# A selective-scan and expert kernel: deeper product ring, spread row scatters, sums kept in the output, and products with zeros on TensorE

## The reference, cut to what matters

```
h = layernorm(x) * (1 + ca) + sa                       # x: 8 sequences x 512 tokens x 256
xn = h * rsqrt(mean(h*h) + eps) * norm_w
xi, z = split(xn @ W_in)                               # 512 channels each
xc = silu(causal_conv(xi, 4 taps) + conv_b)
dt, Bm, Cm = split(xc @ W_x)                           # 64, 16, 16
dt = softplus(dt @ W_dt + b_dt)
h_s[t] = exp(dt*A_s) * h_s[t-1] + dt*xc*Bm[:, s]       # 16 states s, a scan over the 512 tokens
y = sum_s h_s * Cm[:, s] + D_skip * xc
x = x + ga * (h + (y * silu(z)) @ W_out)
h = layernorm(x) * (1 + cb) + sb
w, idx = top_2_of_8(h @ Wg), softmaxed
out_e = relu(xhat_e @ W1_e + b1_e) @ W2_e + b2_e + h   # only the two chosen experts count
x = x + gb * sum_of_two(w * out_e)
```

## Time and profile before

| what | value |
|---|---|
| median of three runs | 1634.65 us |
| profiled execution | 1636.39 us, span 1634.1 us |
| PE, DVE, POOL, ACT busy, share of the span | 81%, 76%, 65%, 48% |
| scan stage (73 to 1161 us): DVE busy | 958.7 of 1088 us |
| late tiles (1200 to 1600 us): PE busy | 397.2 of 400 us |

### The profile page before, as it was taken

The page is one execution under the profiler, slowest core; times in us unless marked ns, Lnnn a source line. Parts: engine busy times, 40 slices in busy tenths (PEclk is TensorE's granted clock), DMA queues, the critical chain, the costliest instruction groups (busy, mean ns, idle before and its releaser), DMA issues.

```text
span 1634.1 us, 25818 instructions
## 1 busy us (share of the span) xinstructions
PE 1329.9 (81%) x7954; PEld 1081.0 (66%) x7954; DVE 1237.3 (76%) x2161; ACT 786.4 (48%) x1378; POOL 1054.4 (65%) x942
## 2 busy tenths in 40 slices
PE   4567786777777887887888788778799999999994
PEld 1245465455556665665666566767689999999993
DVE  3798999989979889889998987789355555555552
ACT  2666768757857766775776586476000000000000
POOL 2485887998797898889789687978324352212221
PEclk7797998998989989889888988889999999999997
DMA  6212131321233344334144132944957797667664
GB/s 224 68 52 76 51 56 53 110 74 57 91 103 104 89 145 110 99 112 139 66 120 143 43 108 97 260 149 130 332 158 201 205 270 206 203 201 200 204 185 138
DMA packets 129471, 221.83 MB, mean 136 GB/s; under 512 B 17052, under 2 KB 74920, under 8 KB 129080
## 3 DMA queue, kind: packets, MB, share of 16 engines
q1 hardware_dynamic: 110376, 186.34, 37.3%
q0 software_dynamic: 16064, 28.53, 7.2%
q10 hardware_dynamic: 2896, 5.31, 1.1%
HBM read 182.79 MB, written 41.54 MB: 137 GB/s over the span
## 4 chain that ended last, share of the span: by engine, by line
PE 41%; DVE 20%; POOL 15%; issue 11%; ACT 8%; DMA 2%; SPq 1%; DVEq 0%; POOLq 0%; ACTq 0%
PE psum L1673 12%; PE psum L1689 12%; POOL dBu L873 10%; DVE w_sb L1974 10%; PE psum L1491 5%; DVE y L1985 3%; PE psum L1500 2%; ACT psum L1125 2%; POOL gT L727 2%; POOL rows_d L791 2%; PE psum L1629 2%; ACT hc L1109 1%; PE psum L1642 1%; PE psum L1480 1%; DVE xc L1955 1%
## 5 line engine op out<-in xcount | busy, mean ns | idle before, releaser
L873 POOL TENSOR_TENSOR dBu<-w_sb,brep 128x512 f32<-128x512 f32 x512 | 650.9, 1345 | 65.4 <-DVE w_sb L1974 54.1
L1974 DVE TENSOR_TENSOR_SCAN w_sb<-psum,dBu 128x512 f32<-128x512 f32 x512 | 612.0, 1210 | 93.8 <-ACT psum L1125 46.0
L1491 PE MATMUL psum<-ident,w_sb 128*128 128x128 f32 x2048 | 312.0, 301 | 153.2 <-DVE y L1985 101.1
L1125 ACT ACTIVATE psum<-w_sb,aneg 128x512 f32<-128x512 f32 x512 | 347.6, 692 | 179.3 <-DVE w_sb L1974 176.4
L1491 PEld LDWEIGHTS psum<-ident,w_sb 128*128 128x128 f32 x2048 | 253.3, 154 | 232.2 <-DVE y L1985 144.3
L860 POOL DMA_INDIRECT sum_d<-dBu,token x59 | 92.3, 1564 | 307.7 <-DVE dBu L2196 286.1
L1109 ACT ACTIVATE hc<-psum,ct 128x512 f32<-128x512 f32 x256 | 174.7, 682 | 114.8 <-PE psum L1491 87.4
L1500 PE MATMUL psum<-ident,hc 128*128 128x128 f32 x1024 | 178.1, 308 | 47.8 <-ACT hc L1109 36.4
L1500 PEld LDWEIGHTS psum<-ident,hc 128*128 128x128 f32 x1024 | 138.5, 159 | 92.3 <-ACT hc L1109 62.9
L1985 DVE SCALAR_TENSOR_TENSOR y<-psum,ct,y 128x512 f32<-128x512 f32 x240 | 174.2, 726 | 14.1 <-PE psum L1491 13.7
L1673 PE MATMUL psum<-xgT,win 128*128 128x128 f32 x960 | 112.2, 275 | 1.8 <-issue 1.8
(11 more groups left out here) (264 smaller groups left out, 1758.2 us busy)
## 6 DMA issues: line engine op xcount, KB each, us to landing
brep<-b_d SPq DMA_DIRECT2D x128, 256.0 KB, 3.6
win<-in_W SPq DMA_DIRECT2D x30, 1024.0 KB, 5.0
expert_pieces<-in_W SPq DMA_DIRECT2D x29, 1024.0 KB, 5.0
expert_pieces<-in_W SPq DMA_DIRECT2D x42, 512.0 KB, 5.2
dBu<-rows_d SPq DMA_DIRECT2D x35, 257.0 KB, 2.8
w_sb<-in_W SPq DMA_DIRECT2D x8, 1024.0 KB, 12.9
xg<-rows_d SPq DMA_DIRECT2D x22, 257.0 KB, 2.8
h_d<-hmod SPq DMA_DIRECT2D x8, 512.0 KB, 2.9
```

The costliest lines, as they stand in the source:

```text
L873: nc.gpsimd.tensor_tensor(dBu[:, i % RING, :], u[p][:, c, :], brep[:, s % 4, :], ALU.mult).then_inc(s_dBu, 1)
L1125: nc.scalar.activation(dA[:, i % DA_RING, :], dt[p][:, c, :], ACT.Exp, scale=aneg[:, c, s:s + 1]).then_inc(s_dA, 1)
L1491: last = nc.tensor.transpose(T[:, i // DT, c * P:(c + 1) * P], hs[s % 2][:, c, i * P:(i + 1) * P], ident[:, :])
L1974: nc.vector.tensor_tensor_scan(hs[s % 2][:, c, :], dA[:, i % DA_RING, :], dBu[:, (n * UNITS + i) % RING, :], 0.0, ALU.mult, ALU.add).then_ ...
```

## The change

It has four parts.

1. `RING` goes from 6 to 9.
2. POOL's `send_rows` of a sequence is spread. Two of the eight scatters stood at the end of step 15 and six in steps 0, 1 and 2. Now two stand in each of steps 0, 1, 4 and 5. The early `tile_out` of step 4 goes to step 6. On SP, `load_gate` goes from step 6 to step 9, and for n = 3 `tile_rows` from step 6 to step 7.
3. The tensor `sum_d` is gone. Bases are stored into `out`, and the accumulating scatters go to `out` with a bounds check that drops the filling rows. The last copies, and the zeroing of the spare rows at the start, are gone.
4. PE issues `add_zeros(count)`: float32 products of a 128x128 block of zeros with 512 columns of ones, which are added to PSUM bank 7. They stand at two places of a step, ahead of `states(n, s, 1)` and ahead of `add_up(n, s, 1)`, wherever `occupied` says that the step holds no other matmul there. Counted over the program there are 212 of them: 40 for n = 0, 34 each for n = 1 and 2, 20 each for n = 3 to 6, and 24 for n = 7.

```diff
-RING = 6
+RING = 9
@@ SP
-                sp.dma_start(rows(sum_d, n), x1[:, :, :]).then_inc(s_bast, 16)
+                sp.dma_start(rows(out, n), x1[:, :, :]).then_inc(s_bast, 16)
-                    if 3 <= n <= 6 and s == 6:
+                    if 3 <= n <= 6 and s == (7 if n == 3 else 6):
                         tile_rows(t)
                         tile_pieces(t, (0, 1, 2))
-                    if n >= 1 and s == 6:
+                    if n >= 1 and s == 9:
                         load_gate(n - 1)
-                for n in range(0, NB, 2):
-                    store_out(sp, n)
-                sp.wait_ge(s_out, 16 * NB)
+                sp.wait_ge(s_bast, 16 * NB)
@@ POOL
-                pool.indirect_dma_start(sum_d, bass.IndirectOffsetOnAxis(ap=token[:, i % XR:i % XR + 1], axis=0),
-                                        ysl[:, i % YR, :], None, compute_op=ALU.add).then_inc(s_st, 16)
+                pool.indirect_dma_start(out, bass.IndirectOffsetOnAxis(ap=token[:, i % XR:i % XR + 1], axis=0),
+                                        ysl[:, i % YR, :], None, bounds_check=NTOK - 1, oob_is_err=False, compute_op=ALU.add).then_inc(s_st, 16)
...
                     if n >= 2 and s == 0:
+                        send_rows(n - 2, 0, (0, 1))
+                    if n >= 2 and s == 1:
                         send_rows(n - 2, 0, (2, 3))
-                    if n >= 2 and s == 1:
+                    if n >= 2 and s == 4:
                         send_rows(n - 2, 1, (0, 1))
-                    if n >= 2 and s == 2:
+                    if n >= 2 and s == 5:
                         send_rows(n - 2, 1, (2, 3))
-                    if 4 <= n <= 7 and s == 4:
+                    if 4 <= n <= 7 and s == 6:
                         tile_out(t - 1)
...
-                    if has_o and s == 15:
-                        send_rows(n - 1, 0, (0, 1))
@@ ACT
-                act.wait_ge(s_st, 16 * TILES)
-                for n in range(1, NB, 2):
-                    store_out(act, n)
@@ PE
+            def add_zeros(count):
+                for i in range(count):
+                    nc.tensor.matmul(YT[:, DT + 1, :], zeros[:, :], ones[:, :].unsqueeze(1).to_broadcast([P, DT * 2, P]),
+                                     start=False, stop=False, skip_group_check=True)
+            def occupied(n, s, second):
+                has_o, has_p, has_t = n > 0, n < NB - 1, 3 <= n <= 6
+                if second:
+                    return (has_o and s in (2, 3, 4) or has_p and s in (7, 12, 13) or has_t and s in (6, 8, 14, 15)
+                            or n == NB - 1 and s in (2, 3, 5, 6, 10, 11, 13, 14))
+                return (has_p and s in (2, 3, 4, 5, 8, 12, 13) or has_t and s in (7, 9, 15)
+                        or n == NB - 1 and s in (3, 4, 6, 7, 11, 12, 14, 15))
...
+                    if s > 1 and not occupied(n, s, False):
+                        add_zeros(2)
                     states(n, s, 1)
...
+                    if s > 0 and not occupied(n, s, True):
+                        add_zeros(4 if s == 5 else 2)
                     if s > 0:
                         add_up(n, s, 1)
```

More of the change, by code:

```diff
@@ L62, in adaln_kernel @@
     h_d = dram("h_d", (NTOK, D))
-    sum_d = dram("sum_d", (NTOK + P, D))
     ctx = ExitStack()
@@ L81, in adaln_kernel, with program @@
         YT = psum[:, 4:8, :]
-        program(nc, ctx, sem, ident, tab, psum, T, dA, Q, MOD_PS, YT, mod_d, b_d, h_d, rows_d, sum_d, out,
+        program(nc, ctx, sem, ident, tab, psum, T, dA, Q, MOD_PS, YT, mod_d, b_d, h_d, rows_d, out,
                 x, norm_w, W_in, conv_w, conv_b, W_x, W_dt, b_dt, A_log, D_skip, W_out, Wg, cT, wmod,
                 gamma, beta, W1, b1, W2, b2)
-def program(nc, ctx, sem, ident, tab, PS, T, dA, Q, MOD_PS, YT, mod_d, b_d, h_d, rows_d, sum_d, out,
+def program(nc, ctx, sem, ident, tab, PS, T, dA, Q, MOD_PS, YT, mod_d, b_d, h_d, rows_d, out,
             x, norm_w, W_in, conv_w, conv_b, W_x, W_dt, b_dt, A_log, D_skip, W_out, Wg, cT, wmod,
@@ L169, in program @@
         lower = sb("lower", [P, P])
+        zeros = sb("zeros", [P, P])
         ones = sb("ones", [P, P])
@@ L205, in program @@
         m8n = gT[0:NB, 0, 0:2 * D].rearrange("p (a d) -> p a d", a=2)
-        zrow = hc[:, 0, 0:D]
         def two_of(t):
@@ L212, in program @@
         xs_of = [xin[:, :, :], two_of(xc)[0], *two_of(u), *two_of(dt), *two_of(sz)]
-        s_zero = sem("spare_rows_zeroed")
         s_w = sem("weights_loaded")
@@ L330, in program @@
         s_yb = sem("late_tile_y_with_bias")
-        s_out = sem("out_stored")
         X0_PS = PS[:, 0:4, :]
@@ L415, in expert_on @@
             return eng.value_load(tab[0:1, 0, t:t + 1], min_val=0, max_val=E - 1)
-        def store_out(eng, n):
-            eng.dma_start(out[n * L:(n + 1) * L, :].rearrange("(p i) d -> p (i d)", p=P),
-                          sum_d[n * L:(n + 1) * L, :].rearrange("(p i) d -> p (i d)", p=P)).then_inc(s_out, 16)
         block = own.enter_context(nc.Block())
@@ L566, in prologue @@
                 sp.wait_ge(s_modst, 32)
-                sp.wait_ge(s_const, 1)
-                sp.dma_start(sum_d[NTOK:NTOK + P, :], zrow).then_inc(s_zero, 16)
                 store_h(1)
@@ L657, in _ @@
         def _(pool):
-            pool.memset(zrow, 0.0)
             pool.memset(mhalf[:, :], -0.5)
@@ L662, in _ @@
             pool.memset(used[:, :], 0.0)
+            pool.memset(zeros[:, :], 0.0)
             for k in range(2):
@@ L851, in tile_out @@
                 after(pool, s_st, 16 * t)
-                pool.indirect_dma_start(sum_d, bass.IndirectOffsetOnAxis(ap=idx[:, t % 2:t % 2 + 1], axis=0),
-                                        ysb[:, :], None, compute_op=ALU.add).then_inc(s_st, 16)
+                pool.indirect_dma_start(out, bass.IndirectOffsetOnAxis(ap=idx[:, t % 2:t % 2 + 1], axis=0),
+                                        ysb[:, :], None, bounds_check=NTOK - 1, oob_is_err=False, compute_op=ALU.add).then_inc(s_st, 16)
             def late_out(t):
@@ L946, in epilogue @@
                 tile_out(BEGIN - 1)
-                send_rows(NB - 2, 0, (2, 3))
                 gate(NB - 1, 1)
+                send_rows(NB - 2, 0)
                 send_rows(NB - 2, 1)
@@ L999, in store_base @@
                 act.wait_ge(s_base, n + 1)
-                act.dma_start(sum_d[n * L:(n + 1) * L, :].rearrange("(i p) d -> p i d", p=P), x1[:, :, :]).then_inc(s_bast, 16)
+                act.dma_start(out[n * L:(n + 1) * L, :].rearrange("(i p) d -> p i d", p=P), x1[:, :, :]).then_inc(s_bast, 16)
             def mod_copy(j):
@@ L1278, in prologue @@
                     z_first(c)
-                act.wait_ge(s_zero, 16)
             def body(n, p, has_o, has_p, has_r):
```

## The result

The changed kernel takes 1662.22 us (median of four runs, 1656.06 to 1665.77), the kernel before 1636.2 us in the runs beside it. The ratio is 1.0163, 95% interval 1.0138 to 1.0188: **26 us slower**, where 52 us faster was forecast (1583 us) and even the range ended at 1606. The execution of the trace took 1665.77 us, the longest of the four.

A forecast was written before the change was run, and what follows sets the result against it. DVE's last scan was taken to end the scan stage, with 101 us of its waits to win; PE bounds the late stage. 1636.4 - 14.5 - 22 - 15 = 1584.9 us for the profiled execution, so 1583 us, range 1560 to 1606.

The forecast's parts named there:

- part 3: End of the span: without the last copies the kernel ends after the last scatter lands, 14.5 us less.
- parts 1 and 2: Scan stage: deeper ring and moved scatters cut DVE's 27.3 us of waits behind POOL, 22 us less.
- part 4: Scan stage: products with zeros raise PE's clock and shorten DVE's waits behind PE, net 15 us less.
- The checked scatter: Late stage: the bounds check was taken at no cost; 1.55 us on POOL, about 4.0 us to land.
- Rival D: Late stage: a checked scatter link takes longer than a late tile's 7.25 us; about 1687 us at 9 us; chance 0.04.
- at full clock they fit: Scan stage: 212 products with zeros take 106 us at full clock, where PE has 237 us free.
- rival C: Scan stage: PE becomes the bound, products with zeros delay DVE by 0.9 us a place, 1693 us; chance 0.06.
- The clock: Scan stage: PE's mean granted clock, 0.89 before, should be above 0.95.
- the mechanism: Scan stage: products with zeros hold the clock up, and DVE's 28.1 us of waits behind PE shrink by 16.
- the sign that I had named for a false mechanism: Scan stage: the clock rises and DVE's waits behind PE, 28.1 us before, don't shrink.
- the stalls of the earlier trace: Scan stage: DVE waits behind PE at half clock, one of 3.00 us in step 6 of sequence 3.
- taken off a fifth: Scan stage: of DVE's 27.3 us behind POOL, a fifth was taken off for DVE then waiting on ACT, leaving 22.

The follow-up runs named there:

- run 10: The whole changed kernel, products with zeros included, with the residual's first half kept in PSUM: 1638.48 us, ratio 0.9998 to the kernel before.
- run 7: The changed kernel with each product with zeros on 128 columns, not 512; number and places kept: 1616.24 us, ratio 0.9854 to the kernel before.
- run 11: The kernel before with spread scatters, the end's change, ring of six, residual's first half in PSUM and quarter-length products with zeros: 1606.31 us, ratio 0.9818.
- run 39: Not a run's label but a count: the unchanged kernel before was run 39 times beside the experiments; 1636.2 us in the runs beside the changed kernel.
- run 3: The kernel before with only the end's change (sums kept in `out`, checked scatters, no last copies); ring of six, old scatters: 1624.9 us, ratio 0.9925.
- run 1: The changed kernel without its 212 products with zeros: 1616.53 us, ratio 0.9891 to the kernel before.
- run 6: As run 1, with the residual's first half kept in PSUM, so the addition has one SBUF input: 1609.15 us, ratio 0.981.
- run 12: As run 3, with the residual's first half kept in PSUM: 1622.14 us, ratio 0.9916 to the kernel before.
- run 9: The kernel before with the end's change, a ring of nine, old scatters and the residual's first half in PSUM: 1621.18 us, ratio 0.9898.
- run 2: The kernel before with only the 212 products with zeros added: 1679.47 us, ratio 1.0258.

## Why the prediction was wrong

The terms as the runs have them are -12 (part 3), -8.4 (parts 1 and 2) and +45.7 (part 4), where the sum had -14.5, -22 and -15. Nearly all of the miss is part 4.

**Part 3, right.** -14.5 us in the trace; 12 in the runs.

**The checked scatter, right.** It takes 1.55 us and lands in 4.0 in the median, as before, and a late tile still takes 7.25 us. Rival D did not happen.

**Part 4, the step that failed**: "A 128x512 float32 product takes 1.98/4 = 0.5 us at full clock". The `x4` in the earlier trace rows counts records, and a float32 product leaves two. I had the means to see it: the half of an early tile (L1629) stands as `x8` in the order of PE and as `x16` in the earlier trace rows, and the output projection as `x4` in that order and as `x8` in the trace of before:

```profile
647.82 1.89 PE L1523 MATMUL psum<-wout,gT 128*128 128x256 f32 x8
```

So the price is 0.94 us a product at full clock, and 206 us in the stage (412 records, the rest lies outside) instead of 106. The sum counted 1 us of cost for this, since "at full clock they fit". Free time of PE over a stage says nothing on that: PE is busy 937 of 1088 us, so time is still free, and yet the products delayed the transposes that ACT and DVE wait for. The measured cost is 45.7 us on 106 pairs, 0.43 us a pair. (They stand at 99 places, not 106, since seven places have two pairs.) That is rival C, which put the point where nothing is left at 0.35 us a pair, and which I gave 0.06. Its condition, "if the clock stays at 0.5", was wrong with the same factor of two: at full clock a pair already takes 1.9 us. And its sign, PE busy over 1000 us in the stage, did not show.

**The clock.** Forecast above 0.95 in the stage; it was 0.94, and 0.96 in run 10. The first half of the mechanism (products with zeros raise the clock) holds. The second (DVE's waits behind PE shrink with it, 16 us) does not: together they went from 28.1 to 33.7 us (4.0 for the scan, 29.7 for y), which is the sign that I had named for a false mechanism. Runs 7 and 11 have a clock higher by 0.03 at a third of the PE time and gain nothing that can be told from zero. Of the stalls of the earlier trace rows, the first stood at full clock in the changed kernel and was no shorter (3.45 us), and the second stood again beside a fallen clock (3.28). What a rise of the clock alone would be worth stays open, since both runs change the clock and PE's work together. It may be more than nothing. The kernel before was run 39 times beside the experiments, its clock over the whole span lay between 0.900 and 0.916, and the time went against it: the 12 executions at 0.913 or more took 1629.8 to 1637.9 us, the 5 at 0.903 or less 1640.4 to 1643.7. Which is cause and which effect, these numbers don't say.

**Parts 1 and 2, half right.** Forecast -22 us, measured -8.4 (run 3 to run 1). The stalls behind POOL went (35.7 to 8.3 us), but the scatters did all of it, and I had let both share one sum. On top, the addition that the ring lengthens was a cost that I had no line for. From run 3 to run 1 it grew from 14.7 to 25.2 us for 14, and taking the hold away (run 6) gives 7.4 us back. The rest is missing without it too: with the residual in PSUM, parts 1 and 2 bring 13.0 us (run 12 to run 6), not 22. I had taken off a fifth for waits that turn into others. From run 3 to run 1 the DVE waits that PE ended, for scan and y, rose from 23.2 to 31.3 us, which may be that rest; it was not tested. In the changed kernel the 14 additions took 31.1 us, and in step 3 of sequences 3 to 6, from one `y` to that of the next step, 14.4 to 14.8 us, where the kernel before has 9.3 to 10.6 and run 10 has 9.3 in all four.

The trace of before held the sign. All 14 additions are of one shape, with a median of 691 ns and a longest of 1986, though no row names a wait inside them. A longest of three times the median is what I passed over. The Trainium skill, "SBUF — State Buffer", section "Who interferes with whom", says that a DVE instruction with two SBUF inputs and a GpSimd instruction that reads SBUF exclude each other, the later one blocked until the earlier has finished. The runs agree that it takes two SBUF inputs (0.69 us with one, run 9). But the rule as written would hold the addition for one product, 1.3 us. Here it took 6.07 us, beyond the end of a whole row of four, although it had started 0.6 us before that row.

The price of the zeros depends on the rest: 45.7 us with the residual in SBUF and 29.3 in PSUM (run 6 to run 10). One way is that a late TensorE shifts the addition into POOL's rows: in sequence 3 it takes 5.80 us in the changed kernel and 0.69 in run 1. That is at most 5 of the 16 us, and run 2 speaks against it as the whole, since there the zeros cost 42.7 us with additions no longer than before (1047 and 1043 ns). The rest stays open.

## What to carry to other kernels

Read what one instruction costs from a place where the code says how many there are, for a profile can count records. Idle time of an engine over a stage is no room for filler work. Price it per place, by who is queued behind it, and try a quarter of its length first. A deeper ring lets the producer run without gaps, so before deepening look for consumer instructions with two SBUF inputs beside it, and compare their longest with their median.

## What the hardware showed that I had not expected

- A 128x512 float32 product on PE takes 0.94 us at full clock and 1.9 us at half (3.76 us for two). It leaves two MATMUL records (424 for the 212 products with zeros).
- A DVE addition of two SBUF tensors of 128x512 takes 0.69 us alone and up to 6.16 us beside POOL products that read SBUF without a gap. It ends about 0.55 us after POOL's row. With one input in PSUM it takes 0.69 us beside them. The DVE scans and the additions of y, each with one input in PSUM, kept their 1.21 and 0.73 us.
- The clock fell to 1.2 GHz in a stretch where PE was busy for every us, 0.5 us into a pair of 512-column products with zeros that followed 8-column products.
